# A two-layer network of convolution, mixing and routed low-rank layers on one core: the second layer's low-rank rows are turned by ScalarE and VectorE instead of TensorE

## The reference

```python
x = x + _L1_ffn_ref(_L1_cond_ref(x, cond_128, ...), base_W, gate_W, lora_A, lora_B)

# _L1_cond_ref: per sample a 64 x 64 matrix, mixed of 8, over the channels
att = softmax(h @ W2 + b2)
agg_w = einsum('bk,koi->boi', att, weight)
out = einsum('boi,bih->boh', agg_w, x) + (att @ bias_k)[:, :, None]

# _L1_ffn_ref: 28 experts of rank 8, of which each row takes two
base = xf @ base_W.T                                  # 1024 x 1024
logits = xf @ gate_W.T                                # 28 columns
top_vals, top_idx = top_k(logits, 2)
gate_full = zeros((N, 28)).at[arange(N)[:, None], top_idx].add(softmax(top_vals))
h = einsum('nd,erd->ner', xf, lora_A)                 # 28 x 8 = 224 columns
h = h * (gate_full * 2.0)[:, :, None]
lora_out = einsum('ner,eor->no', h, lora_B)           # from 224 to 1024
out = base + lora_out
```

## Time and profile before

| | |
|---|---|
| three runs | 1205.23, 1207.8, 1211.32 us; median 1207.8 |
| profiled execution | 1200.46 us, span 1198.5 us, granted clock 0.998 |
| TensorE (PE) busy | 1171.6 us, 98% of the span |
| ScalarE (ACT) busy | 767.6 us |
| VectorE (DVE) busy | 706.4 us |
| GpSimd (POOL) busy | 297.5 us |
| second layer | from 562.8 us to the end |

### The profile page before, as it was taken

One profiled execution on the slowest core, in us unless ns is written; L12 is line 12 of the kernel. 1 busy time (PEld: TensorE's weight loads), 2 busy tenths in 40 slices (PEclk: granted clock), 3 DMA queues, 4 the chain that ended last, 5 costly groups with the idle time before them and its releaser, 6 DMA issues.

```text
span 1198.5 us, 22055 instructions
## 1 busy us (share of the span) xinstructions
PE 1171.6 (98%) x6783; PEld 1034.3 (86%) x6783; DVE 706.4 (59%) x1985; ACT 767.6 (64%) x1746; POOL 297.5 (25%) x315
## 2 busy tenths in 40 slices
PE   6999999999999999999999999999999999999998
PEld 6999999999899999898787787787788888888887
DVE  6677778777465655557764444454445555555552
ACT  5566667666586776864667767767645665755751
POOL 4111733323222223234312112111131222222200
PEclk9999999999999999999999999999999999999999
DMA  9566566775999999979699999999875455455410
GB/s 333 185 241 258 191 225 229 285 268 165 253 319 327 311 322 311 325 269 242 127 245 304 268 293 311 281 292 299 269 165 118 99 123 110 118 123 118 110 53 36
DMA packets 84698, 267.15 MB, mean 223 GB/s; under 512 B 23248, under 2 KB 27472, under 8 KB 77360
## 3 DMA queue, kind: packets, MB, share of 16 engines
q1 hardware_dynamic: 72608, 230.12, 58.4%
q0 software_dynamic: 11600, 36.06, 17.0%
q10 hardware_dynamic: 432, 0.30, 0.1%
HBM read 154.24 MB, written 112.20 MB: 222 GB/s over the span
## 4 chain that ended last, share of the span: by engine, by line
PE 41%; DMA 7%; SPq 1%; issue 1%; DVE 1%; ACT 1%; POOL 0%; ACTq 0%; POOLq 0%; DVEq 0%
PE z L1461 12%; PE z L1462 12%; PE z L1463 12%; DMA ht<-hs_dram 3%; DMA xin<-zs_dram,gpos 2%; DMA xin<-x_dram 1%; PE c L1461 1%; PE c L1463 1%; PE c L1462 1%; PE c L1528 1%; PE prep L1725 1%; DMA x<-zs_dram,gpos 1%; DVE xb L1433 1%; PE c L1532 1%; PE c L1530 1%
## 5 line engine op out<-in xcount | busy, mean ns | idle before, releaser
L754 ACT ACTIVATE moved<-mid 32x256 f32<-32x256 f32 x944 | 392.2, 415 | 139.0 <-DVE mid L1023 114.6
L1461 PE MATMUL z<-w_1h,yh 128*128 128x384 f32 (+1 forms) x512 | 190.0, 371 | 0.0
L1461 PE MATMUL z<-w_0h,yh 128*128 128x384 f32 (+1 forms) x512 | 187.4, 366 | 0.2 <-DVE xb L1433 0.2
L1463 PE MATMUL z<-w_1l,yh 128*128 128x384 f32 (+1 forms) x512 | 185.8, 363 | 0.0
L1463 PE MATMUL z<-w_0l,yh 128*128 128x384 f32 (+1 forms) x512 | 185.8, 363 | 0.0
L1462 PE MATMUL z<-w_1h,yl 128*128 128x512 f32 (+1 forms) x504 | 183.0, 363 | 0.0
L1462 PE MATMUL z<-w_0h,yl 128*128 128x512 f32 (+1 forms) x504 | 182.8, 363 | 0.0
L669 POOL TENSOR_TENSOR carrier<-ones_col 128x1 f32<-128x1 f32 x96 | 25.5, 266 | 539.1 <-DVE den L1117 131.8
L1461 PE MATMUL z<-w_2h,yh 128*128 128x336 f32 (+1 forms) x512 | 152.9, 299 | 2.1 <-DVE yl L1031 2.1
L1463 PE MATMUL z<-w_2l,yh 128*128 128x336 f32 (+1 forms) x512 | 152.5, 298 | 0.0
L1462 PE MATMUL z<-w_2h,yl 128*128 128x252 f32 (+1 forms) x504 | 149.9, 297 | 0.0
(11 more groups left out here) (217 smaller groups left out, 2587.8 us busy)
## 6 DMA issues: line engine op xcount, KB each, us to landing
bd<-bd_dram SPq DMA_DIRECT2D x96, 512.0 KB, 9.0
zs_dram<-zt SPq DMA_DIRECT2D x96, 512.0 KB, 10.2
hs_dram<-zt SPq DMA_DIRECT2D x34, 512.0 KB, 6.6
x8raw<-in_x_dram SPq DMA_DIRECT2D x32, 516.0 KB, 4.4
xin<-in_x_dram SPq DMA_DIRECT2D x32, 512.0 KB, 6.9
x_dram<-xb SPq DMA_DIRECT2D x32, 512.0 KB, 5.2
out_dram<-xb SPq DMA_DIRECT2D x32, 512.0 KB, 4.7
bd_dram<-bd SPq DMA_DIRECT2D x8, 1024.0 KB, 6.5
```

Of the source, the lines that this page charges most:

```text
L754: return nc.scalar.activation(o, i_, ACT.Copy)
L1461: T.matmul(o, ah, wh, start=start, stop=False, **kw)
L1463: return T.matmul(o, ah, wl, start=False, stop=stop, **kw)
```

## The change

`hx1` gets two halves of 128 columns, of which 128 and 96 are used. ScalarE copies its blocks of 32 x 32 to the quadrant that is theirs after the transposition (`hx_moves`, into `hx_moved`): for each of four quadrants of source partitions and four of destination one copy, of 32 partitions x 2 x 32 elements, or 32 x 32 where only the first half has the block. VectorE transposes within the blocks with one instruction (`turn_hx`, into `hx_turned`), and `h1h` and `h1l` are made from that. The two transpositions on TensorE go, and `over_h` runs over 128 and 96 rows. `lb` is laid out for that, with spare rows of zeros.

In ScalarE's program the sixteen copies stand between `mixed_out` and the moves, `h1h` between the two halves of the moves, and the second half of the moves behind it and, in tiles 2 to 13, behind the first two outputs `zt`. In late tiles and in the last one the copies stand ahead of `h1h`. In VectorE's program `turn_hx` and `hx_low` stand ahead of `turn_rows`.

```diff
+            def hx_moves(t):
+
+                act.wait_ge(a1.hx, 3 * t + 2)
+                act.wait_ge(a1.hT_ps, t)
+                for q in range(P // Q):
+                    for i in range(P // Q):
+                        k = 2 if Q * i < K1[1] else 1
+                        mm = copy(hx_moved[Q * i:Q * (i + 1), 0:k, Q * q:Q * (q + 1)],
+                                  hx1[Q * q:Q * (q + 1), 0:k, Q * i:Q * (i + 1)])
+                mm.then_inc(a1.hx, 1)
+
+            def hx_high(t):
+
+                act.wait_ge(a1.hT_ps, t + 1)
+                copy(h1h[:, :, :], hx_turned[:, :, :]).then_inc(a1.hT_hi, 1)
...
                 exps(a1, t)
                 if not last and not late:
                     mixed_out(t + 1)
-                    for part in range(2):
-                        moves(a1, t + 1, part)
+                    hx_moves(t)
+                    moves(a1, t + 1, 0)
+                    hx_high(t)
                 if late:
                     act.wait_ge(a1.c_ps[1], t + 1)
                     x1_high(t + 1, i + (v + 1) // 4, (v + 1) % 4)
                     mix_high(t + 1)
+                if late or last:
+                    hx_moves(t)
                 if first:
                     w1_high(1, w1_pieces(1)[2:4])
                     act.wait_ge(lb_in, 16)
...
                     outputs(s, 0, cp)
                     outputs(s, 1, tp)
-                act.wait_ge(a1.hT_ps, t + 1)
-                copy(h1h[:, :, :], prepp[0:K1, 0:2 * P].rearrange("p (k r) -> p k r", r=P)).then_inc(a1.hT_hi, 1)
+                if late or last:
+                    hx_high(t)
+                else:
+                    moves(a1, t + 1, 1)
...
+            def turn_hx(t):
+                dve.wait_ge(a1.hx, 3 * t + 3)
+                V.transpose(hx_turned[:, :, :].rearrange("p k (q r) -> p (k q) r", r=Q),
+                            hx_moved[:, :, :].rearrange("p k (q c) -> p (k q) c", c=Q)).then_inc(a1.hT_ps, 1)
+
+            def hx_low(t):
+                dve.wait_ge(a1.hT_hi, t + 1)
+                V.tensor_tensor(h1l[:, :, :], hx_turned[:, :, :], h1h[:, :, :], ALU.subtract).then_inc(a1.hT_lo, 1)
...
+                turn_hx(t)
+                hx_low(t)
+                if not late and not last:
                     turn_rows(a1, tiles)
-                dve.wait_ge(a1.hT_hi, t + 1)
-                V.tensor_tensor(h1l[:, :, :], prepp[0:K1, 0:2 * P].rearrange("p (k r) -> p k r", r=P),
-                                h1h[:, :, :], ALU.subtract).then_inc(a1.hT_lo, 1)
...
-                for k in range(ah.shape[1]):
-                    mm = three(z[b][:, 0:w.stop - w.start], ah[:, k, :], al[:, k, :], wh[:, k, w], wl[:, k, w],
-                               False, k == ah.shape[1] - 1, skip_group_check=True)
+                for k, n in enumerate(K1):
+                    mm = three(z[b][:, 0:w.stop - w.start], ah[0:n, k, :], al[0:n, k, :], wh[0:n, k, w], wl[0:n, k, w],
+                               False, k == len(K1) - 1, skip_group_check=True)
...
-                pe.wait_ge(a1.hx, 2 * t + 2)
                 if tables:
                     pe.wait_ge(tab_ready, 4)
-                for k in range(2):
-                    mm = T.transpose(prepp[0:K1, P * k:P * (k + 1)], hx1[:, K1 * k:K1 * (k + 1)], ident[:, :])
-                mm.then_inc(a1.hT_ps, 1)
```

More of the change, by code:

```diff
@@ L46 @@
 ER1 = E1 * R1
-K1 = ER1 // 2
+K1 = (128, ER1 - 128)
 GC = E1 + ER1
@@ L177, in build @@
         hl = sb(ctx, "hl", [2 * R0, PER // 2, P], F32R)
+        hx_moved = sb(ctx, "hx_moved", [P, 2, P])
+        hx_turned = sb(ctx, "hx_turned", [P, 2, P])
         mbrow = sb(ctx, "mbrow", [P, 1])
@@ L208, in build @@
         x1_2 = sb(s, "x1_2", [P, L])
-        hx1 = sb(s, "hx1", [P, ER1])
+        hx1 = sb(s, "hx1", [P, 2, P])
         s.close()
@@ L215, in build @@
         w1raw[1], w1l[1] = raw_and_low(s, "w1_1", [P, KC, W1B[1]])
-        lbraw, lbl = raw_and_low(s, "lb", [K1, 2, L])
+        lbraw, lbl = raw_and_low(s, "lb", [P, 2, L])
         s.close()
@@ L222, in build @@
         w1h[1] = sb(s, "w1_1h", [P, KC, W1B[1]], F32R)
-        lbh = sb(s, "lbh", [K1, 2, L], F32R)
+        lbh = sb(s, "lbh", [P, 2, L], F32R)
         s.close()
@@ L251, in build @@
         s = ExitStack()
-        h1h = sb(s, "h1h", [K1, 2, P], F32R)
-        h1l = sb(s, "h1l", [K1, 2, P], F32R)
+        h1h = sb(s, "h1h", [P, 2, P], F32R)
+        h1l = sb(s, "h1l", [P, 2, P], F32R)
         s.close()
@@ L928, in _ @@
             step0(TILES - 2, 0)
-            act.wait_ge(mix_zero, 2)
+            act.wait_ge(mix_zero, 3)
             mix_high(0)
@@ L1121, in spread1 @@
                 V.tensor_tensor(comb[:, 0:E1], comb1[:, 0:E1], comb2[:, 0:E1], ALU.add).then_inc(a1.hx, 1)
-                dve.wait_ge(a1.hx, 2 * t + 1)
-                V.tensor_tensor(hx1[:, :].rearrange("p (e r) -> p e r", r=R1),
+                dve.wait_ge(a1.hx, 3 * t + 1)
+                V.tensor_tensor(hx1[:, :, :].rearrange("p k n -> p (k n)")[:, 0:ER1].rearrange("p (e r) -> p e r", r=R1),
                                 z[2][:, SM1 + E1:SM1 + GC].rearrange("p (e r) -> p e r", r=R1),
@@ L1353, in _ @@
                 V.memset(m[:, :].bitcast(U32), 0).then_inc(mix_zero, 1)
-            dve.wait_ge(mix_zero, 2)
+            V.memset(hx_moved[K1[1]:P, 1, :], 0.0).then_inc(mix_zero, 1)
+            dve.wait_ge(mix_zero, 3)
             mix(0)
@@ L1795 @@
     b0 = v["L0_ffn_B"].transpose(0, 2, 1)
-    lb = v["L1_ffn_lora_B"].reshape(2, E1 // 2, L, R1).transpose(1, 3, 0, 2)
+    lb = _np.pad(v["L1_ffn_lora_B"].transpose(0, 2, 1).reshape(ER1, L), ((0, 2 * P - ER1), (0, 0))).reshape(2, P, L)
     mix = _np.tile(v["L1_cond_weight"].reshape(MIX, C, C).transpose(2, 0, 1), (2, 1, 1))
@@ L1803 @@
         "cW2": v["L1_cond_W2"], "cb2": v["L1_cond_b2"], "mix": mix.reshape(P, MIX * C), "mix_b": v["L1_cond_bias_k"],
-        "w1": w1.reshape(P // Q, KC, Q, L + GC).transpose(0, 2, 1, 3).reshape(P, KC, L + GC), "lb": lb.reshape(K1, 2, L),
+        "w1": w1.reshape(P // Q, KC, Q, L + GC).transpose(0, 2, 1, 3).reshape(P, KC, L + GC), "lb": lb.transpose(1, 0, 2),
     }
```

## The result

The changed kernel takes 1266.9 us (median of four runs, 1261.5 to 1269.6) against 1209.1 us for the kernel before (four runs, 1205.2 to 1211.3): 1.049 times as long, interval 1.046 to 1.052. The forecast was 1258, with 1230 to 1290 as its range. The profiled execution took 1268.22 us (span 1266.3, granted clock 0.982).

What follows compares the result with a forecast made beforehand. TensorE, 98% busy, bounds the kernel before; ScalarE's copies would make the tile-to-tile loop the bound. Its terms sum to +50.4 us: 1200.46 becomes 1251 profiled, with 7.3 to the median 1258, range 1230 to 1290.

Steps and rivals of the forecast that it cites:

- TensorE's pair: Second layer, TensorE: dropping its two transpositions gives back 0.22 us per tile, 7 us over 32 tiles if TensorE stays the bound.
- Sixteen copies: ScalarE, ahead of the moves: the added copies to `hx_moved` take 4.03 us per tile, bounds 2.4 to 6.8.
- New wait for `hx`: ScalarE, ahead of the copies: they wait about 0.62 us for `hx`, semaphore included.
- Transposition and its reader: VectorE: its transposition and the reading of `hx_turned` lie in its 4.5 us wait for the moves and cost nothing.
- Plain tile: Second layer, tiles without listed pairs (1, 14, 16 to 30): from 18.17 us to a loop of 19.95 us.
- List tile: Second layer, tiles with listed pairs (2 to 13): from 21.86 us to a loop of 23.4 us.
- Tiles 2 to 13: Second layer, tiles with listed pairs: eleven of them add 17.0 us, the first still has slack and adds 0.3.
- Tiles 16 to 30: Second layer, fifteen tiles without listed pairs: each goes from 18.17 to 19.95 us, together 26.7 us more.
- The clock: Rival, TensorE: new waits lower its clock, 16 tiles lose up to 1.7 us more each, +27 us, 1285; chance 0.06.
- main case: Whole kernel: the copies lengthen the loop beyond TensorE's work; 1258 us, its own range 1243 to 1273, chance 0.73.
- `h1h` in the middle: ScalarE: `h1h` between the halves of the moves stands ahead of VectorE's transposition, costing about 0.40 us per tile.
- Only the first order: Rival, second layer: the delay of `yl` does not reach `lg`, VectorE's 1.38 us idle absorbs it; 1233 us, chance 0.09.

Runs made afterwards that it cites:

- e5: The changed kernel with eight of the sixteen copies, zeros in place of the others: 1203.9 us, 0.9974 of the kernel before.
- e6: The changed kernel with twelve of the sixteen copies, zeros in place of the others: 1228.8 us, 1.017 times the kernel before.
- e2: The kernel before without TensorE's pair of transpositions, `h1h` reading whatever stands in the bank: 1202.7 us, 0.9973 of the kernel before.
- e7: The changed kernel's order and sixteen copies, but TensorE's pair turns the rows and nobody reads the copies: 1259.5 us, 1.046 times the kernel before.
- e8: The changed kernel with the copies behind the first half of the moves in tiles 16 to 30: 1250.4 us, 1.036 times the kernel before.
- e4: The changed kernel with the first residual sum `xb` ahead of `turn_rows` in tiles 16 to 30: 1263.9 us, 1.048 times the kernel before.
- e9: The changed kernel with five unused matmuls per tile ahead of TensorE's wait for `yl`, from tile 16 on: 1259.7 us, 1.046 times the kernel before.

## Why the prediction was right

- *What bounds:* right. TensorE in the earlier trace rows, and a loop of 14.9 us with 3.3 of slack behind it. e5 and e6 show the slack: 2.07 us of copies are free beside the wait for `hx` and `h1h`, 3.1 are not.
- *TensorE's pair, 0.22 us per tile:* 0.27 (e2). It did not come back as time in plain and list tiles, as forecast.
- *Sixteen copies, 4.03 us and no overlap:* 4.14 (255 and 227 ns). The row it was nearest to, the moves, decided rightly between 2.4 and 6.8. The overlap of 93 ns that the Trainium skill states (ScalarE: Activation LUTs, What ACT_TABLE_LOAD costs), by which with the same section's price of one the copies would have taken an estimated 2.2 us, does not appear between these copies.
- *New wait for `hx`, 0.62:* 0.74.
- *Transposition and its reader at nothing:* right (e7).
- *Plain tile 19.95:* 20.02. *List tile 23.4:* 23.45. *Tile 14 +1.8:* 1.85. *Tiles 0 and 1 +5:* 5.5.
- *Tiles 2 to 13 +17.3:* 17.3, in part by luck. The first of them, priced at +0.3, took 3.6 more, and the other eleven 13.7 and not 17.0. In tile 2 the clock fell, and ahead of the `yl` for which tile 3 waits VectorE had other work from 637.90 to 640.56, while `yh` was begun at 637.41; before, `yl` there was early enough (begun at 620.83 for a tile that began at 625.26). Some of the eleven had been longer than 21.86 before (tile 5: 23.11).
- *Tiles 15 and 31 -0.2 each:* -0.2 and +1.4. In 31 the clock fell (wait 1.86 us, granted clock 0.57 in its first 4 us).
- *Tiles 16 to 30 +26.7:* 27.8 for the loop, 34.9 in all. Here a step failed. The clock was set against the main case as a rival that excludes it, with a chance of 0.06 and 1.7 us in every plain tile. It came together with it, in six or seven of 15 tiles, at 1.1 us. The prediction had named a falling clock as a sign that it was wrong. In the traces the second layer grew by 60.8 us where 50.4 were forecast, and 7.1 of these 10.4 us are the clock in tiles 16 to 30, 1.6 more tile 31. The waits fell just where the two rows of before differed: that was an argument for half a price in the sum, not for a small chance.
- *`h1h` in the middle as a cost of 0.40:* it does stand on the path (0.42, 1115.61), but the step did not ask what the old place would cost. The second path, `h1h`, `h1l`, `over_h`, was left out. That it did no harm to the forecast was luck: in the plain tile above `h1l` is done at 1116.06 + 0.43 = 1116.49 and `over_h` begins at 1116.93, 0.4 us later. It made two expectations miss by 58 and 76 us.
- *Only the first order (1233):* false. Plain tiles would be 19.3; they are 20.02, with no idle time ahead of `lg`.

## What to carry to other kernels

An engine that is idle for a third of the time can still be without room: follow the loop from one tile to the next through all engines in program order, and compare its length with the bound engine's tile; work is free up to the difference and costs its full time after it. Count every path that starts at the moved work, the one to this tile's end as well as the one to the next tile's beginning. Where TensorE comes to wait once per tile for longer than the waits after which the clock was seen to stay, put a fallen clock in some of the tiles into the sum, and not only among the rivals.

## What the hardware showed

- TensorE's clock fell from 2.4 to 1.2 GHz at the beginning of tiles after some waits of 1.61 to 2.16 us and not after others (spacing in the first matmuls 0.21 and not 0.12 us). In the changed kernel it fell in seven tiles from 16 to 31 after 1.86 to 2.16 and in tile 2 after 2.01, and not at 641.39, 1121.80 and 1224.16 after 2.03, 1.89 and 1.88; in e8 it did not fall at 641.56 after 2.79. In e4 it fell after six of fourteen waits of 1.61. In the traces of e6 to e9 no plain tile's clock fell, after waits of 1.59 or less. So between 1.6 and 2.8 us a wait's length alone doesn't decide, and what does is not shown. In the changed kernel and e4 no two tiles in a row fell, though in e4 the wait behind a fallen tile was 1.61 again.
- Sixteen copies of 32 partitions follow each other on ScalarE at 0.26 us, none overlapping (the mean duration is 0.25), while `mixh` starts 0.09 us before `x1h` ends. From 64 and 32 elements per partition to 256 the price goes from 0.25 and 0.23 to 0.415 us: by an estimate from the straight line through 32 and 256 elements about 0.20 us of each doesn't depend on its size.
